# Explicit drains taken away from most VectorE and ScalarE instructions of a layer-norm, windowed-attention and mixture-of-experts kernel

## The reference

```
xn  = (x - mean) / sqrt(var + 1e-5)                 # x: 8 x 2048 x 1024
out = x + attention(xn) + experts(xn)

attention: qkv = xn @ w_qkv.T + b; 16 heads of 64; windows of 256 queries that see
           512 keys (128 to each side), positions outside the sequence masked;
           softmax, times v, @ w_proj.T + b_proj
experts:   8 experts, top 2 of softmaxed gate logits;
           act = (xn @ w0.T + b0) * silu(xn @ w1.T + b1)   # 1024 -> 2048
           out = sum over the two of weight * (act @ w2.T + b2)
```

## Time and profile before

| | us |
|---|---|
| median of 2 runs (3863.28 and 3885.28) | 3874.28 |
| the profiled execution, device time | 3866.41 |
| its span on the slowest core (core 3), from first to last instruction | 3863.8 |
| spans of the 8 cores | 3819.8 to 3863.8 |
| PE busy on core 3 | 3158.8 (82%) |
| VectorE busy | 1120.2 (29%) |
| ScalarE busy | 598.0 (15%) |

### The profile page before, as it was taken

One profiled execution on the slowest core, in us unless ns is written; L12 is line 12 of the kernel. 1 busy time (PEld: TensorE's weight loads), 2 busy tenths in 40 slices (PEclk: granted clock), 3 DMA queues, 4 the chain that ended last, 5 costly groups with the idle time before them and its releaser, 6 DMA issues.

```text
span 3863.8 us, 40486 instructions; the slowest of 8 cores (3819.8 to 3863.8 us)
## 1 busy us (share of the span) xinstructions
PE 3158.8 (82%) x15136; PEld 1437.6 (37%) x15136; DVE 1120.2 (29%) x1913; ACT 598.0 (15%) x1031; POOL 257.4 (7%) x300
## 2 busy tenths in 40 slices
PE   2395333337599989999999999999999999999990
PEld 0142122224144434444444444444444444444440
DVE  4644222224322322231232224123322422332242
ACT  0001344441011011101100110110011011001100
POOL 0010000000011001001100110110011011001000
PEclk6697555558699999999999999999999999999995
DMA  3340000001443053315314430641333053233205
GB/s 117 82 49 1 1 1 1 1 1 23 62 48 38 7 72 39 33 18 70 39 16 68 38 37 1 87 39 17 66 39 39 1 82 39 22 66 39 28 1 174
DMA packets 310592, 154.47 MB, mean 40 GB/s; under 512 B 285296, under 2 KB 287728, under 8 KB 305272
## 3 DMA queue, kind: packets, MB, share of 16 engines
q0 software_dynamic: 305056, 118.05, 26.0%
q1 hardware_dynamic: 5344, 33.83, 2.6%
HBM read 252.53 MB, written 8.45 MB: 68 GB/s over the span
## 4 chain that ended last, share of the span: by engine, by line
PE 79%; DMA 7%; ACT 6%; DVE 4%; issue 3%; ACTq 0%; DVEq 0%; POOL 0%; SPq 0%; POOLq 0%
PE pb L716 23%; PE pb L674 22%; PE pb L680 22%; ACT exp L529 6%; DMA w1sl<-w1T 3%; PE pb L519 3%; PE pb L381 3%; DMA xs<-xT 2%; PE pb L540 2%; PE pb L414 1%; PE pb L599 1%; DVE SUM L622 1%; PE pb L617 0%; DVE xsq L286 0%; DVE ob L749 0%
## 5 line engine op out<-in xcount | busy, mean ns | idle before, releaser
L674 PE MATMUL pb<-xn,w0sl 128*128 128x512 bf16 x4096 | 979.9, 383 | 66.7 <-DMA w1sl<-w1T 52.3
L680 PE MATMUL pb<-xn,w1sl 128*128 128x512 bf16 x4096 | 969.8, 380 | 0.0
L716 PE MATMUL pb<-act,W2T 128*128 128x512 bf16 x4096 | 887.0, 379 | 15.6 <-DVE act L695 15.6
L695 DVE SCALAR_TENSOR_TENSOR act<-pb,b0cols,sil 128x512 bf16<-128x512 f32 x512 | 384.4, 751 | 1469.5 <-ACT sil L689 1469.5
L689 ACT ACTIVATE sil<-pb,b1cols 128x512 bf16<-128x512 f32 x512 | 352.9, 689 | 2271.1 <-PE pb L680 2271.1
L674 PEld LDWEIGHTS pb<-xn,w0sl 128*128 128x128 bf16 x4096 | 402.2, 98 | 561.2 <-issue 87.5
L716 PEld LDWEIGHTS pb<-act,W2T 128*128 128x128 bf16 x4096 | 400.6, 98 | 502.0 <-issue 21.5
L680 PEld LDWEIGHTS pb<-xn,w1sl 128*128 128x128 bf16 x4096 | 401.6, 98 | 486.6 <-issue 6.1
L721 DVE TENSOR_TENSOR tmpb<-pb,gwb 128x512 f32<-128x512 f32 x256 | 177.1, 692 | 527.5 <-PE pb L716 527.5
L540 PE MATMUL pb<-V,exp 128*128 128x65 bf16 x960 | 73.1, 240 | 305.8 <-ACT exp L529 305.8
L529 ACT ACTIVATE exp<-pb,c_shift 128x256 bf16<-128x256 f32 x480 | 228.7, 477 | 287.6 <-PE pb L519 262.4
(11 more groups left out here) (66 smaller groups left out, 572.8 us busy)
## 6 DMA issues: line engine op xcount, KB each, us to landing
w0sl<-w0T POOLq DMA_DIRECT2D x128, 256.0 KB, 4.5
w1sl<-w1T POOLq DMA_DIRECT2D x128, 256.0 KB, 5.5
W2T<-w2T POOLq DMA_DIRECT2D x8, 4096.0 KB, 29.2
xs<-xT SPq DMA_DIRECT2D x24, 1024.0 KB, 6.2
gwb<-gw_scratch POOLq DMA_DIRECT2D x8, 1024.0 KB, 30.1
outT<-ob SPq DMA_DIRECT2D x8, 1024.0 KB, 4.7
qksl<-wqkvT POOLq DMA_DIRECT2D x16, 256.0 KB, 4.4
vsl<-wqkvT POOLq DMA_DIRECT2D x2, 1024.0 KB, 15.4
```

What stands on the lines that cost most here:

```text
L674: step("tensor", lambda t, s=slot, dt=dt, tc=tc, par=par: t.matmul(pb[par * 2][:], w0sl[s][:, dt * 128:(dt + 1) * 128], xn[dt][:, tc * 512 ...
L680: h_mm_done[(e, ht)] = step("tensor", lambda t, s=slot, dt=dt, tc=tc, par=par: t.matmul(pb[par * 2 + 1][:], w1sl[s][:, dt * 128:(dt + 1) * ...
L695: act_evac[(e, i)] = step("vector", lambda v, ht=ht, tc=tc, par=par, bcol=bcol: v.scalar_tensor_tensor(out=act[ht][:, tc * 512:(tc + 1) * ...
L716: b_last_mm = step("tensor", lambda t, ht=ht, dt=dt, tc=tc, bk=bk: t.matmul(pb[bk][:], W2T_sb[:, ht * D + dt * 128:ht * D + dt * 128 + 128 ...
```

## The change

`finalize` no longer drains ahead of every operation. `step` gets a parameter `dr`, off by default, that marks an operation to have a drain ahead of it. It is set on the VectorE operations that read what the VectorE operation just before them wrote (the statistics' chain, L351 and L352, the gate's chain, L481, L551, L723). No ScalarE operation has it: L322, L453, L455, L529 and L689 lose their drain. On VectorE L265 to L267, L285, L286, L392, L420, L426, L444, L476, L549, L586, L606, L622, L695, L721 and L749 lose it. The reciprocals `rc` of even and odd iterations get columns of their own (4 instead of 2). In `barrier` the `nop` that increments the counter becomes a `drain` on all five engines; on VectorE and ScalarE this takes the place of a drain and a `nop`.

```diff
-    rc_sb = sb("rc", [128, 2], F32, o); o += 32
+    rc_sb = sb("rc", [128, 4], F32, o); o += 32
...
-    def step(eng, fn, ctr=None):
+    def step(eng, fn, ctr=None, dr=False):
+        kind = "op_dr" if dr else "op"
         if ctr is None:
-            rec.emit(eng, fn)
+            rec.emit(eng, fn, kind=kind)
             return None
...
-        rec.emit(eng, lambda E, f=fn, s=sem: f(E).then_inc(s, 1))
+        rec.emit(eng, lambda E, f=fn, s=sem: f(E).then_inc(s, 1), kind=kind)
...
-            rec.emit(e, lambda E, s=sem: E.nop(nofuse=True).then_inc(s, 1))
+            rec.emit(e, lambda E, s=sem: E.drain().then_inc(s, 1))
...
-        def run(E, name, drain_ops=False):
+        def run(E, name):
             for kind, f in rec.ops[name]:
-                if drain_ops and kind == "op":
+                if kind == "op_dr":
                     E.drain()
                 f(E)
...
-                run(v, "vector", drain_ops=True)
+                run(v, "vector")
...
-                run(s, "scalar", drain_ops=True)
+                run(s, "scalar")
...
-                step("vector", lambda v, abk=abk, qi=qi: v.reciprocal(
-                    rc_sb[:, qi:qi + 1], pb[abk][:, qi * 65 + 64:qi * 65 + 65]))
-                ev = step("vector", lambda v, abk=abk, qi=qi, g=g, h=h: v.tensor_scalar(
+                rcc = par * 2 + qi
+                step("vector", lambda v, abk=abk, qi=qi, rcc=rcc: v.reciprocal(
+                    rc_sb[:, rcc:rcc + 1], pb[abk][:, qi * 65 + 64:qi * 65 + 65]))
+                ev = step("vector", lambda v, abk=abk, qi=qi, g=g, h=h, rcc=rcc: v.tensor_scalar(
                     out=AO[g * 2 + qi][:, h * 64:(h + 1) * 64],
                     in0=pb[abk][:, qi * 65:qi * 65 + 64],
-                    scalar1=rc_sb[:, qi:qi + 1], scalar2=None, op0=ALU.mult),
-                    cv if qi == 1 else None) or ev
+                    scalar1=rc_sb[:, rcc:rcc + 1], scalar2=None, op0=ALU.mult),
+                    cv if qi == 1 else None, dr=True) or ev
```

More of the change, by code:

```diff
@@ L310, in build_program @@
         step("vector", lambda v, sl=sl, c=c: v.tensor_scalar(
-            out=m_b[:, sl], in0=pb[c][:], scalar1=1.0 / D, scalar2=None, op0=ALU.mult))
+            out=m_b[:, sl], in0=pb[c][:], scalar1=1.0 / D, scalar2=None, op0=ALU.mult), dr=True)
         if LVL < 2:
             continue
-        step("vector", lambda v, sl=sl: v.tensor_tensor(st_a[:], m_b[:, sl], m_b[:, sl], ALU.mult))
+        step("vector", lambda v, sl=sl: v.tensor_tensor(st_a[:], m_b[:, sl], m_b[:, sl], ALU.mult), dr=True)
         ve_done = step("vector", lambda v, c=c: v.scalar_tensor_tensor(
             out=st_b[:], in0=pb[4 + c][:], scalar=1.0 / D, in1=st_a[:],
-            op0=ALU.mult, op1=ALU.subtract), cv)
+            op0=ALU.mult, op1=ALU.subtract), cv, dr=True)
         if LVL < 3:
@@ L326, in build_program @@
         rec.wait("vector", cs, sq_done)
-        step("vector", lambda v: v.reciprocal(st_d[:], st_c[:]))
+        step("vector", lambda v: v.reciprocal(st_d[:], st_c[:]), dr=True)
         if LVL < 5:
             continue
-        step("vector", lambda v: v.tensor_tensor(st_a[:], st_d[:], st_d[:], ALU.mult))
+        step("vector", lambda v: v.tensor_tensor(st_a[:], st_d[:], st_d[:], ALU.mult), dr=True)
         step("vector", lambda v: v.scalar_tensor_tensor(
-            out=st_c[:], in0=st_a[:], scalar=-0.5, in1=st_b[:], op0=ALU.mult, op1=ALU.mult))
+            out=st_c[:], in0=st_a[:], scalar=-0.5, in1=st_b[:], op0=ALU.mult, op1=ALU.mult), dr=True)
         stats_done = step("vector", lambda v, sl=sl: v.scalar_tensor_tensor(
-            out=r_b[:, sl], in0=st_c[:], scalar=1.5, in1=st_d[:], op0=ALU.add, op1=ALU.mult), cv)
+            out=r_b[:, sl], in0=st_c[:], scalar=1.5, in1=st_d[:], op0=ALU.add, op1=ALU.mult), cv, dr=True)
     if debug_upto == "p0m_m":
@@ L350, in build_program @@
         rec.wait("vector", dxs[slot], xload[slot])
-        step("vector", lambda v, s=slot: v.tensor_tensor(xtmp[:], xs[s][:], m_b[:], ALU.subtract))
-        xfree[slot] = step("vector", lambda v, dt=dt: v.tensor_tensor(xn[dt][:], xtmp[:], r_b[:], ALU.mult), cv)
+        step("vector", lambda v, s=slot: v.tensor_tensor(xtmp[:], xs[s][:], m_b[:], ALU.subtract), dr=True)
+        xfree[slot] = step("vector", lambda v, dt=dt: v.tensor_tensor(xn[dt][:], xtmp[:], r_b[:], ALU.mult), cv, dr=True)
     if debug_upto == "p0":
@@ L448, in build_program @@
         sl = slice(tt * 8, (tt + 1) * 8)
-        step("vector", lambda v, sl=sl: v.max(out=m8_sb[:], in_=l_sb[:, sl]))
+        step("vector", lambda v, sl=sl: v.max(out=m8_sb[:], in_=l_sb[:, sl]), dr=True)
         mx_done = step("vector", lambda v: v.tensor_scalar(
-            out=negm1[:], in0=m8_sb[:, 0:1], scalar1=-1.0, scalar2=None, op0=ALU.mult), cv)
+            out=negm1[:], in0=m8_sb[:, 0:1], scalar1=-1.0, scalar2=None, op0=ALU.mult), cv, dr=True)
         rec.wait("scalar", cv, mx_done)
@@ L458, in build_program @@
         step("vector", lambda v: v.tensor_scalar(
-            out=den_sb[:], in0=e1_sb[:], scalar1=1.0, scalar2=None, op0=ALU.add))
-        step("vector", lambda v: v.reciprocal(rden_sb[:], den_sb[:]))
+            out=den_sb[:], in0=e1_sb[:], scalar1=1.0, scalar2=None, op0=ALU.add), dr=True)
+        step("vector", lambda v: v.reciprocal(rden_sb[:], den_sb[:]), dr=True)
         step("vector", lambda v, sl=sl: v.tensor_scalar(
-            out=mask_sb[:], in0=l_sb[:, sl], scalar1=m8_sb[:, 1:2], scalar2=None, op0=ALU.is_ge))
+            out=mask_sb[:], in0=l_sb[:, sl], scalar1=m8_sb[:, 1:2], scalar2=None, op0=ALU.is_ge), dr=True)
         gw_done = step("vector", lambda v, sl=sl: v.scalar_tensor_tensor(
             out=gw_sb[:, sl], in0=p8_sb[:], scalar=rden_sb[:], in1=mask_sb[:],
-            op0=ALU.mult, op1=ALU.mult), cv)
+            op0=ALU.mult, op1=ALU.mult), cv, dr=True)
     gwt_evac = 0
@@ L480, in build_program @@
     gwT_hbm_done = dma("sync", dgww, gw_hbm[:], gwT_sb[:])
-    gwTb_done = step("vector", lambda v: v.tensor_copy(gwTb_sb[:], gwT_sb[:]), cv)
+    gwTb_done = step("vector", lambda v: v.tensor_copy(gwTb_sb[:], gwT_sb[:]), cv, dr=True)
     if debug_upto == "p1q":
@@ L724, in build_program @@
                     SUM[dt][:, tc * 512:(tc + 1) * 512], SUM[dt][:, tc * 512:(tc + 1) * 512],
-                    tmpb[j % 2][:], ALU.add), cv)
+                    tmpb[j % 2][:], ALU.add), cv, dr=True)
         if e + 1 < NE:
```

## The result

The changed kernel takes 3788.7 us against 3884.3 us (medians over all executions; in some of either kernel one die ran at a lower clock, and the ratio leaves those out). The ratio is 0.978, 95% interval 0.975 to 0.981: about 2.2% faster, clear of no change, though the interval reaches across 2%. The profiled execution took 3788.8 us where that of before took 3866.4, 77.6 less; the forecast was 68.8 less.

What follows compares the result with a forecast made beforehand. TensorE was taken to bound the experts and a chain of dependent work attention. Terms, led by 55.3 us from exponentials, summed to 68.8 us off the profiled 3866.4, giving 3798 us; range 3765 to 3835.

Steps and rivals of the forecast that it cites:

- Where the bound is: Whole kernel: TensorE bounds the experts' 2763 us; a chain of dependent work, not an engine, sets attention's 498 us.
- Exponentials: Attention: 352 exponentials directly behind another lose a 0.067 us gap and overlap by 0.09 us, 55 us gained.
- My test for the start-to-start: Attention: the prediction is wrong if successive exponentials do not start between 0.38 and 0.41 us apart.
- the one that a duration mustn't change with its neighbours: Attention: the prediction is wrong if the duration of one exponential, about 0.477 us, changes with its neighbours.
- Rival A: One engine's instructions never overlap and a drain costs only its gap: 35 us gained, 3831 us; chance 0.12.
- rival B: Attention's exponentials start at the full streaming rate, 0.212 us apart: 132 us gained, 3735 us; chance 0.08.
- Drains after a wait: Drains on an engine idle after a wait cost 0.04 us each, 5.1 us over attention's 128 iterations.
- Gate, transposes, b2, experts, output: Small gains: gate 2.6 and 0.6 us, transposes' copies 0.6, b2's turns 1.3, experts 0.9, output 0.3.
- Statistics and VectorE's pairs: Statistics: L285 and L286 on VectorE gain 0.18 us eight times, 1.4 us, including an overlap of 0.07 each.
- Projection: Shorter transposes and copies only lengthen TensorE's wait for `wp`, 0 us gained; the last four copies gain 0.5 us.
- Rival C: TensorE's clock rises to its upper level in attention: 96 us more gained, 3702 us; chance 0.04.
- Rival D: Experts' waits for transfers grow by 69 us and take the gain back, some 3875 us; chance 0.03.

Runs made afterwards that it cites:

- The two experiments: Changed kernel with drains put back only between an iteration's exponentials (attention 488.6 us), and only ahead of its first exponential (attention 431.3 us).
- ahead_wide: Changed kernel with the next iteration's scores ahead of the products and one exponential for two score blocks; 3565.9 us, ratio 0.920 to the kernel before.

## Why the prediction was right, point by point

- *Where the bound is.* Right: experts unchanged (2733.8 and 2733.1 us), attention a chain on one engine after another.
- *Exponentials.* Right in mechanism; the term was under-sized. I took an overlap of 0.09 us between two engines' rows, 0.063 and 0.163; it is 0.102, 0.110 and 0.118 between the four. That the value lay so near was in part luck: nothing in those two rows says where between them ScalarE's would be. The stage lost 62.0 us (drains put back) to 64.6 us (summed over the trace) by it, in place of 55. My test for the start-to-start, 0.38 to 0.41, failed: it is 0.362. So did, by 0.008 us, the one that a duration mustn't change with its neighbours (0.467 to 0.483, where all took 0.474 to 0.477 before). The term was the weakest of the sum, since no row of before could show it, and its bounds of 24 and 117 us held it. The Trainium skill's 93 ns ("ScalarE: Activation LUTs", What ACT_TABLE_LOAD costs) is near but low here: 102 to 118 ns with 256 columns. Rival A, no overlap, and rival B, full streaming rate, are both out, by the row of 1.57 us for four.
- *Drains after a wait.* Right: 0.04 forecast; 4.7 us / 128 = 0.037 with the other drains gone, and (496.4 - 488.6) / 128 = 0.061 with them in place. In the change itself it is 5.7 / 128 = 0.045. The two experiments together leave 3.1 us of the stage. The trace shows where these lie: with the other drains in place the drain after the wait is worth 6.0 us against 4.9 without them, and 1.3 us more fall between the first and the last exponential. Why is open.
- *Gate, transposes, b2, experts, output.* Right within a microsecond each.
- *Statistics and VectorE's pairs.* Under-sized by 0.7 us. A slice's period fell by 0.22 us (7.47 to 7.25) and not 0.18; the rest of the 2.1 us are slices in which TensorE's sums took 3.2 to 3.5 us and not 3.57, in both kernels, which isn't the drains' doing. VectorE overlaps too: the row below (changed kernel, core 4) has the square start 0.08 before the cast's end, where the earlier trace rows had it 0.07 after.

```profile
23.58 1.23 DVE L286 CAST xb<-xs 128x2048 bf16<-128x2048 f32 x1 [3.83 <-PE pb L295]
24.73 2.28 DVE L287 TENSOR_TENSOR xsq<-xs 128x2048 bf16<-128x2048 f32 x1
```

  With rival A I gave only half of what the Trainium skill says ("VectorE: DVE Perf Modes", The DRAIN you can't avoid). The same section adds: "A next op that is not held starts earlier", and these independent ones do, by 0.08 us. So the rule told against the rival as much as for it.
- *Projection.* Right that it hardly gains. The transposes took 13.0 us in place of 14.0 (mean of eight cores), and the wait for `wp` grew in the mean from 2.3 to 2.8 us; on core 3 it is 2.3 us where the earlier trace rows had 1.7. The matmuls behind it took 57.0 us against 56.3, and the last copies gave 0.6.
- *Rival C, the clock.* Out, and by more than I argued: it stays at 0.50 in attention with TensorE 44% busy, and even 96% busy with scores ahead and wide exponentials.
- *Rival D, the transfers.* Out: core 4 waits 53.9 us for w1sl, core 3 of before 52.3, each the slowest of its run. The mean of eight cores is 37.5 us after and 39.5 before, and it did depend on how the cores meet: core 3's went from 52.3 to 32.7.
- *The chances.* The profiled 3788.8 us lie in the range of 3765 to 3835. Within 2% was given 0.60 and faster by over 2% 0.38. The result, 0.978, lies on the other side of that line, and its interval reaches across it; I had put the line at an overlap of 0.114. The sum fell short by 9 us, and 7 to 9 of them are the one term above.

## What to carry to other kernels

Price a drain by what stands behind it. Between two instructions that ScalarE could run back to back it cost 0.18 us, three to four times what it cost after a wait (0.04 to 0.06), and it counts only where that engine is on the chain: 480 drains, of the 2298 instructions by which the page's count fell (40486 to 38188), gave 69.5 of the 79 us that the stages add up to. Where the chain goes engine to engine, look at the order of the lists before the price of the instructions: moving the next scores ahead of the products brought 211 us in the stage in which taking away all drains had brought 70.

## What the runs showed of the hardware

- An exponential directly behind the first of a group starts 0.265, 0.373 and 0.586 us after it at 128, 256 and 512 columns, an overlap of 0.10 us at each width; a later one starts 0.250 and 0.357 after the one ahead (128 and 256 columns). That is 0.14 to 0.16 us fixed and 0.83 ns a column.
- TensorE's granted clock stayed at 0.50, the lower level, through a stretch in which it was busy 172.4 of 180 us with matmuls of 64 rows by 256 columns and of 65 columns (ahead_wide). The experts' matmuls of 128 rows and 512 columns ran at 0.99. Busy time alone doesn't say which level is granted. Which property of the attention's matmuls keeps it low wasn't tried.
